# Seven of nine down products a slot, accumulated transposed from high and low parts

## What is computed

```
x = x + 0.5 * ffn_moe(layernorm(x))       # 16 experts of width 64, top 2, and a shared expert of width 128
x = x + linear_attention(layernorm(x))
x = x + 0.5 * ffn_moe(layernorm(x))       # the same weights again
x = x + 0.5 * ffn(layernorm(x))           # width 512, ReLU
```

```
g  = silu(einsum('th,ehi->eti', x, We_gate)); u = einsum('th,ehi->eti', x, We_up)
ye = einsum('eti,eih->eth', g * u, We_down)
y  = einsum('te,eth->th', comb, ye)
shared = silu(x @ Ws_gate) * (x @ Ws_up) @ Ws_down
```

## Time and profile before

| | |
|---|---|
| median of 3 runs | 1980.31 us (1979.03 to 1980.67) |
| the profiled execution, its own time | 1978.75 us |
| its span | 1976.9 us, granted TensorE clock 0.99 on the mean |
| the 32 slots with a side layer | from 70.62 to 1118.07 us of the span |
| the whole front | about the first 1146 us |

### The profile page before, as it was taken

One profiled execution on the slowest core, in us unless ns is written; L12 is line 12 of the kernel. 1 busy time (PEld: TensorE's weight loads), 2 busy tenths in 40 slices (PEclk: granted clock), 3 DMA queues, 4 the chain that ended last, 5 costly groups with the idle time before them and its releaser, 6 DMA issues. The chain is left out here.

```text
span 1976.9 us, 34600 instructions
## 1 busy us (share of the span) xinstructions
PE 1889.2 (96%) x12468; PEld 1308.3 (66%) x12468; DVE 1542.2 (78%) x3888; ACT 1179.2 (60%) x2210; POOL 670.7 (34%) x766
## 2 busy tenths in 40 slices
PE   2999999999999999999999979999999999999997
PEld 2888888888888888888888834444444444444443
DVE  5777776677767766776677679999999999999991
ACT  3344444444444444444444438888888888888884
POOL 2433433343234323432343223333333333333311
PEclk9999999999999999999999969999999999999998
DMA  3000000000000000000010032222222222223210
GB/s 132 7 11 1 12 11 12 1 12 12 12 1 11 12 12 1 12 12 11 1 38 7 6 102 87 87 87 89 91 91 89 90 88 87 87 88 90 87 40 11
DMA packets 49994, 85.83 MB, mean 43 GB/s; under 512 B 6753, under 2 KB 11105, under 8 KB 49761
## 3 DMA queue, kind: packets, MB, share of 16 engines
q1 hardware_dynamic: 47920, 81.85, 13.3%
q10 hardware_dynamic: 1904, 1.78, 0.3%
HBM read 49.26 MB, written 34.87 MB: 43 GB/s over the span
## 5 line engine op out<-in xcount | busy, mean ns | idle before, releaser
L1507 DVE TENSOR_REDUCE b_nm<-b_MX 128x1 f32<-128x512 f32 x1024 | 651.4, 682 | 45.1 <-PE b_MX L1615 27.1
L1400 ACT ACTIVATE b_pr<-b_ST 128x512 f32<-128x512 f32 x1024 | 552.3, 609 | 91.8 <-PE b_ST L1603 89.7
L517 ACT ACTIVATE s<-G 128x512 f32<-128x512 f32 x306 | 182.6, 597 | 293.7 <-PE G L836 289.5
L671 DVE TENSOR_TENSOR su<-U,s 128x512 f32<-128x512 f32 x272 | 187.0, 687 | 208.1 <-PE U L836 105.6
L841 PE MATMUL Y<-w_wd,h 128*128 128x128 f32 x2448 | 327.4, 277 | 4.3 <-DVE h L680 4.3
L841 PEld LDWEIGHTS Y<-w_wd,h 128*128 128x128 f32 x2448 | 308.1, 191 | 26.8 <-DVE h L680 14.7
L1615 PE MATMUL b_MX<-b_kt,b_qt 32*128 32x512 f32 x768 | 236.7, 504 | 2.4 <-DVE b_nm L1507 2.4
L1603 PE MATMUL b_ST<-b_qt,b_kt 32*128 32x512 f32 x768 | 214.7, 494 | 2.7 <-ACT b_pr L1400 1.5
L1603 PEld LDWEIGHTS b_ST<-b_qt,b_kt 32*128 32x128 f32 x768 | 83.1, 181 | 195.1 <-ACT b_pr L1400 140.3
L680 DVE TENSOR_TENSOR h<-C,su 128x512 f32<-128x512 f32 x272 | 188.0, 691 | 9.3
L834 PE MATMUL G<-xh,w_wgh 128*128 128x512 f32 x306 | 145.2, 475 | 0.0
(11 more groups left out here) (295 smaller groups left out, 3697.5 us busy)
## 6 DMA issues: line engine op xcount, KB each, us to landing
b_kt<-staging SPq DMA_DIRECT2D x48, 256.0 KB, 3.1
b_qt<-staging SPq DMA_DIRECT2D x48, 256.0 KB, 3.4
staging<-e_khi SPq DMA_DIRECT2D x32, 256.0 KB, 2.9
staging<-e_qhi SPq DMA_DIRECT2D x32, 256.0 KB, 2.9
xin<-in_x SPq DMA_DIRECT2D x17, 256.0 KB, 2.8
mid<-xo SPq DMA_DIRECT2D x16, 256.0 KB, 2.0
staging<-e_klo SPq DMA_DIRECT2D x16, 256.0 KB, 2.9
staging<-e_qlo SPq DMA_DIRECT2D x16, 256.0 KB, 2.9
```

What stands on the lines that cost most here:

```text
L517: nc.scalar.activation(sbuf_s[n % 2][:], G[n % 2][:], ACT.Silu).then_inc(act_done.sem, 1)
L671: nc.vector.tensor_tensor(out[:], U[:], sbuf_s[n % 2][:], ALU.mult).then_inc(up_used.sem, 1)
L1400: nc.scalar.activation(pr[k % 2][:, j], bank[:].rearrange("p a b -> p (a b)"), ACT.Exp, scale=SM_SCALE).then_inc(used["st"].sem, 1)
L1507: nc.vector.tensor_reduce(nm[g % 2][:, c:c + 1], bank[:].rearrange("p a b -> p (a b)"), AX.X, ALU.max).then_inc(used["mx"].sem, 1)
```

## The change

Tiles 0 to 6 (`NV` = 7) get another down product. ACT copies `h` into `hh` (float32r, the high part), POOL subtracts it, `hl = h - hh` (the low part), and PE adds three matmuls of 512 columns into a new PSUM bank `V`: `wdh` x `hh`, `wdl` x `hh`, `wdh` x `hl`. Here the weights are stationary, so `V` comes out transposed. After tile 6, ACT copies `V` to `vs`, and PE transposes that by four matmuls that accumulate onto `Y`, between the first and the second of the two down products (tiles 7 and 8) that stay as they were. `V` takes the bank of the second `G`, so that a gate product now waits for the `silu` of the tile just before it. Where the down products of tiles 0 and 1 stood in the loop's steps 1 and 2, there is none now; step 3 does tiles 0 and 1, step n from 4 to 7 does tile n - 2, and step 8 does tiles 6 and 7. DVE writes `h` for tile n once `hl` of tile n - 3 is done. The weights' parts `wdh` and `wdl` are made once, at the start.

```diff
+            def low(m, n, i):
+                pool.wait_ge(hh_ready.sem, hh_ready.at(i, NV * m + n + 1))
+                nc.gpsimd.tensor_tensor(hl[n % 3][:], h[n % 3][:], hh[n % 3][:],
+                                        ALU.subtract).then_inc(hl_ready.sem, 1)
...
                 for m in range(NM):
                     side_start(m, i, m)
-                    main_normalise(m + 1, i)
-                    if SIDE[m] == ATT:
+                    if SIDE[m] == MLP:
+                        lows(m, i, (0,))
+                        side_bias(m, i, m)
+                        lows(m, i, (1,))
+                        main_normalise(m + 1, i)
+                        lows(m, i, range(2, NV))
+                    else:
                         a = nth(m)
+                        lows(m, i, (0, 1))
+                        main_normalise(m + 1, i)
+                        lows(m, i, (2,))
+                        side_bias(m, i, m)
+                        lows(m, i, (3,))
...
+            lows(0, turns, range(4))
             pool.wait_ge(early.mv_ready.sem, 1)
...
+            def high(m, n, i):
+                if n == 0:
+                    act.wait_ge(up_used.sem, up_used.at(i, NT * m + 1))
+                else:
+                    act.wait_ge(h_ready.sem, h_ready.at(i, TE * m + n))
+                nc.scalar.activation(hh[n % 3][:], h[n % 3][:], ACT.Copy).then_inc(hh_ready.sem, 1)
...
+                    if 1 <= n <= NV:
+                        high(m, n - 1, i)
                     if n == 1 and side:
                         side_normalise(m, i, m)
...
                 if n >= 3:
-                    dve.wait_ge(down_done.sem, down_done.at(i, g0 + n - 2))
+                    dve.wait_ge(hl_ready.sem, hl_ready.at(i, NV * m + n - 2))
...
+                if n < NV:
+                    high, low = hh[n % 3], hl[n % 3]
+                    pe.wait_ge(hh_ready.sem, hh_ready.at(i, NV * m + n + 1))
+                    pe.matmul(flat(V), w["wdh"][:, n], flat(high), start=(n == 0), stop=False, skip_group_check=True)
+                    pe.wait_ge(hl_ready.sem, hl_ready.at(i, NV * m + n + 1))
+                    pe.matmul(flat(V), w["wdl"][:, n], flat(high), start=False, stop=False, skip_group_check=True)
+                    pe.matmul(flat(V), w["wdh"][:, n], flat(low), start=False, stop=True,
+                              skip_group_check=True).then_inc(down_done.sem, 1)
+                    return
...
-                    if n >= 1:
-                        moe_down(m, n - 1, i)
+                    if n == 3:
+                        moe_down(m, 0, i)
+                    if n >= 3:
+                        moe_down(m, n - 2, i)
+                    if n == NT - 1:
+                        moe_down(m, NT - 2, i)
...
                 if prepare:
                     gate(m + 1, 0, i)
+                down_transposes(m, i)
                 moe_down(m, NT - 1, i)
```

More of the change, by code:

```diff
@@ L34 @@
 NT = TE + 1
+NV = 7
 FT = 4
@@ L207, in build_front @@
         h = [sb(f"h{k}", [P, T, P]) for k in range(3)]
+        hh = [sb(f"hh{k}", [P, T, P], F32R) for k in range(3)]
+        hl = [sb(f"hl{k}", [P, T, P], F32R) for k in range(3)]
+        vs = sb("vs", [P, T, P])
         kvu = sb("kvu", [P, T, 3 * D])
@@ L225, in build_front @@
         hs = [sb(f"hs{k}", [P, T, P]) for k in range(2)]
-        G = [ps(f"G{k}", [P, T, P]) for k in range(2)]
+        G = ps("G", [P, T, P])
+        V = ps("V", [P, T, P])
         U = ps("U", [P, T, P])
@@ L399, in main_normalise, with lows, side_bias @@
                 nc.gpsimd.tensor_tensor(z[:], z[:], rstd[:].broadcast_to([P, T, D]), ALU.mult).then_inc(z_ready.sem, 1)
+            def low(m, n, i):
+                pool.wait_ge(hh_ready.sem, hh_ready.at(i, NV * m + n + 1))
+                nc.gpsimd.tensor_tensor(hl[n % 3][:], h[n % 3][:], hh[n % 3][:],
+                                        ALU.subtract).then_inc(hl_ready.sem, 1)
+            def lows(m, i, tiles):
+                for n in tiles:
+                    low(m, n, i)
             def side_start(m, i, k):
                 scale_offset(rstd_s, off_s, vpe_s, mv_s, smv_ready, smv_ready.at(i, k + 1), srstd_ready)
+            def side_bias(m, i, k):
                 pool.wait_ge(side_done.sem, side_done.at(i, k))
@@ L408, in _ @@
             main_normalise(-1, 0)
+            own.step(nc.gpsimd.tensor_tensor(w["wdl"][:], w["wd"][:, 0:NV], w["wdh"][:], ALU.subtract))
+            own.settle()
+            lows(-1, 0, (0, 1))
             main_normalise(0, 0)
+            lows(-1, 0, range(2, NV))
             own.step(nc.gpsimd.memset(early.va[:], 0.0))
@@ L454, in _ @@
             nc.gpsimd.tensor_tensor(early.xn[:], early.xn[:], w["lnsb"][:], ALU.add).then_inc(early.xn_ready.sem, 1)
+            lows(0, turns, range(4, NV))
         @block.scalar
@@ L516, in slot @@
                         act.wait_ge(up_used.sem, up_used.at(i, g0))
-                    nc.scalar.activation(sbuf_s[n % 2][:], G[n % 2][:], ACT.Silu).then_inc(act_done.sem, 1)
+                    nc.scalar.activation(sbuf_s[n % 2][:], G[:], ACT.Silu).then_inc(act_done.sem, 1)
                     if n == 0:
@@ L548, in slot @@
                         first_batch(n)
+                down_copy(m, i)
             main_high(-1, 0)
@@ L845, in moe_down, with down_transposes @@
             def moe_down(m, n, i):
-                if n == 0:
-                    pe.wait_ge(main_done.sem, main_done.at(i, m))
[L849 to L852, removed]
+                if n < NV:
[7 more added lines that the diff above has]
+                    return
+                if n == NV:
+                    pe.wait_ge(main_done.sem, main_done.at(i, m))
+                pe.wait_ge(h_ready.sem, h_ready.at(i, TE * m + n))
+                down(Y, h[n % 3], w["wd"][:, n], n == NV).then_inc(down_done.sem, 1)
+            def down_transposes(m, i):
+                pe.wait_ge(vs_ready.sem, vs_ready.at(i, m + 1))
+                for t in range(T):
+                    pe.matmul(Y[:, t], vs[:, t], w["ident"][:], start=False, stop=True, is_transpose=True,
+                              skip_group_check=True)
             def comb_transposes(m, i):
@@ L953, in gate @@
                 g0 = NT * m
-                if n >= 2:
-                    pe.wait_ge(act_done.sem, act_done.at(i, g0 + n - 1))
-                elif n == 0:
+                if n >= 1:
+                    pe.wait_ge(act_done.sem, act_done.at(i, g0 + n))
+                else:
                     pe.wait_ge(xl_ready.sem, xl_ready.at(i, m + 1))
@@ L1684, in build_weights @@
     sb("wd", [P, NT, D])
+    sb("wdh", [P, NV, D], F32R)
+    sb("wdl", [P, NV, D], F32R)
     for name in ("minus_half", "eps", "eps_two", "both"):
@@ L1819, in _ @@
                 nc.scalar.activation(high, whole, ACT.Copy).then_inc(high_ready, 1)
+            wait_loads(act, "down")
+            nc.scalar.activation(w["wdh"][:], w["wd"][:, 0:NV], ACT.Copy)
             for n, f in enumerate(angle):
```

11 lines of the change are left out of this document (10 added, 1 removed).

## The result

The changed kernel takes 2072.86 us (median of 4, 2069.65 to 2076.76), the kernel before on the same chip 1979.67 us (4, 1977.47 to 1980.67). The ratio is 1.047, with a 95% interval of 1.0453 to 1.0487: 4.7% slower. The profiled execution took 2073.94 us, with a span of 2072.1 us against 1976.9, so 95.2 us are to be found.

What follows compares the result with a forecast made beforehand. PE was taken to bound the kernel, busy 1032.77 of 1047.45 us in the 32 full slots. 16 x (3.0 + 0.6) + 16 x 0.8 + 9 = 79 us on 1978.75 gave 2058 us, range 2010 to 2100.

Steps and rivals of the forecast that it cites:

- PE saves 0.18 a product, 0.43 goes back: PE, every slot: seven cheaper down products save 1.27 us, four transposes onto `Y` cost 0.43; net 0.84 us.
- Nothing is saved up to step 3: ATT slot's start: PE reaches the transposes of `zs` sooner but must wait for the unchanged side-input chain; saving 0.
- `z` late by 2.34: ATT slot: `main_normalise` queues on POOL behind `hl` of tile 1, so PE waits for `z`; +2.34 us.
- The rest of the ATT slot: ATT slot, gate of tile 5 to next slot: +0.37 us of PE work, +0.6 (0 to 3.1) of DVE delays.
- MLP slot +0.8: MLP slot: tile 2's `V` product waits for `hl` behind `z`, more work follows; +0.8 us (0.4 to 1.3).
- Single `G` 0: Every step: the `silu` is over before the next gate product is due; cost 0, at worst 0.3.
- Last slot +8.9: Last slot: `e_xn`'s chain stands behind `hl` of tiles 0 to 3, +6.9 us, and slow clock afterwards, +2.
- Clock: ATT slots, a rival: the clock falls in every slot's pause, PE loses 2 us a slot; 2090 us, chance 0.06.
- Head and first slot at 0: Start: making `wdh`, `wdl` costs nothing; first slot loses about as much at `z` as PE saves; 0.
- Rival 1: All slots: PE's saving of 0.84 us a slot comes through, faster; about 1950 us, chance 0.04.
- Rival 2: `z` in time: POOL gets to `main_normalise` about when it did; ATT slot costs 0.7 us, total 2012, chance 0.14.
- the two SBUF terms: ATT slot: POOL's instructions hold up DVE's, the last `h` 0.5 us late and `en` ahead of `attend` 0.1.

Runs made afterwards that it cites:

- Experiment 8: Against the five-tile kernel of experiments 7: four tiles a slot through `V`, 2 to 5 in ATT slots, 3 to 6 elsewhere; 1960.19 us, 0.9899 of the kernel before.
- Experiment 2: Changed kernel with tile 0's three `V` matmuls moved from step 3 to step 2, ahead of the transposes of `zs`; 2059.43 us.
- Experiment 1: Changed kernel with POOL's low part of tile 1 moved behind `main_normalise` in ATT slots; 2028.19 us.
- Experiment 5: Changed kernel without POOL's subtractions in the slots, the third matmul of a product reading `hh` instead of `hl`; 1994.40 us.
- experiment 4: Kernel before with only one `G` bank, so a gate product waits for the `silu` of the tile just before it; 1979.38 us, ratio 0.9998.
- experiment 6: Changed kernel with POOL's chain of `e_xn` put ahead of all low parts in the last slot; 2070.29 us.
- Experiment 3: Changed kernel with six useless matmuls ahead of the transposes of `z` in ATT slots; 2059.55 us.
- experiments 7: Changed kernel with only tiles 2 to 6 through `V`, `z` made where it was before, `e_xn` ahead of the low parts; 1991.49 us, 1.0059 of the kernel before.
- experiment 9: Changed kernel, seven tiles, with the moves of Experiment 1, Experiment 2 and experiment 6 together; 2007.29 us, 1.0144 of the kernel before.

## Why the prediction was right, and where it was off

The forecast was 2058 us, slower, with 2010 to 2100; the measured 2072.86 lies inside, 15 us above the forecast.

- *PE saves 0.18 a product, 0.43 goes back.* The step of `V` is 0.235 us in the trace, as taken from the gate. Experiment 8, with PE waiting as before, gives 0.20 a product, with the 0.43 taken as given.
- *Nothing is saved up to step 3.* Right: the transposes of `zs` stand at tau 6.71. Experiment 2 shows the hole worth 0.70 us in an ATT slot and nothing in an MLP slot.
- *`z` late by 2.34.* `hl` of tile 1 starts at tau 7.64 (7.74 in the prediction) and `z` ends at 12.45 (12.6), and PE stands 2.04 us. Experiment 1 takes the wait away and 2.25 us a slot with it.
- *The rest of the ATT slot.* From the gate of tile 5 (tau 19.34) to the end are 16.61 us, 0.99 more than before; 0.37 + 0.6 = 0.97 was forecast. The wait for the last `h` is 0.41 us where 0.5 was taken. But both of DVE's instructions beside `hl` and `og` were caught, the case that the prediction priced at 1.8 us; that it cost no more than the case of one was luck. Experiment 5 shows POOL as their cause. Another 0.16 us stands in front of `S<-kvm,qc` (0.1 was forecast behind `en`); it is there without POOL's part too (experiments 5 and 8). The short ATT slot is 35.95 us, 36.0 by my sum.
- *MLP slot +0.8*: it is +0.70, with `z`'s transposes 0.24 us sooner and 0.34 us for tile 2's low part. *Single `G` 0*: experiment 4 shows it. *Last slot +8.9*: +9.2, and experiment 6 gets 6.5 of it back by order alone.
- *Clock: the term that was mis-sized.* I gave the fall of the clock as a rival, all or nothing, in every slot, at 2 us and a chance of 0.06, and put 0 into the sum. As a mechanism the rival was nearly right: the clock fell in 14 of 16 ATT slots. It cost only the 9 in which it fell behind `z`, 1.55 us each: 14 us. Experiment 3 fills the pause, with `z` as late as ever, and the cost is gone. My reason against it, that the pauses are short, rested on no row. The one longer pause in the front of before, 3.99 us in the first slot, could not have told: matmuls ran at 0.43 us a step ahead of it as well as behind it. A term between the two ends would have been due.
- *Head and first slot at 0* were mis-sized too, +3.6 us. The first slot (+1.1) now waits 0.71 us for `silu`, 0.34 us for a low part and 1.28 us for `z` (1.14 before), but in experiment 4, without any of the new work, it took 34.25 us too. The head is not settled: without the new parts of the weights it took 37.20 and 36.24 us (before, experiment 4), with them between 36.92 and 39.86 (nine kernels, mean 38.7), so the build looks like some 1.9 us, beside a spread of its own among kernels that start alike (37.13 to 39.74 in the change and experiments 1, 3 and 6). No run isolates either.

With the clock, and the head and first slot, 79 + 14 + 3.6 = 97 us, against 95.2.

Rival 1 (the saving comes through) broke on the `zs` chain: even without POOL's part the slots stay longer than before (experiment 5). Rival 2 (`z` in time) gave 2012; experiment 1 put `z` in time and got 2028. Rival 2 let the two SBUF terms go with the wait, and they stayed: ATT slots are 1.3 us over before, not 0.7 (10 us in all). The clock behind the stand at `zs` took another 5.6 (5 slots, 1.1 us each), and the rest is the head.

## What to carry to other kernels

On an engine that is 98% busy, mark the few places where it meets another engine's chain. Work that is made cheaper ahead of such a place saves nothing if the chain stands fixed; only what lies behind the last of them counts, and experiments 7 and 8 are the same idea on both sides of that line in MLP slots, where 21 of the 31 us between them lie (33.76 and 32.46 us). Of the ATT slots' 0.5 us, 0.41 is the wait for the last `h`, which went with tile 6, whose low part stood ahead of `og`. When a new instruction is put into an in-order queue, look at what is behind it, not at how busy the engine is: POOL was under 60% full and cost 78 us. And before a stall is priced by its own length, add the clock's fall behind it for some part of the cases, unless the next wait hides it.

## What the runs showed of the hardware

In the changed kernel's ATT slots PE stands twice, 1.34 us for `zs` (1.94 in the first) and then, about 4 us later, for `z`. In 5 of 16 slots the matmuls behind the first stand ran 0.43 us apart. In the other 11 the second stand was 2.03 to 2.05 us, and behind it they ran 0.43 us apart in 9, for up to 3.7 us, and 0.235 us apart in 2. In experiment 2, with no stand at `zs`, a pause of the same 2.04 us did it in 7 of 16. In experiments 1 and 5 the stand of 1.34 us alone did it, in 5 and in 4 of 16, and in experiment 9, with neither stand, none. What decides it from slot to slot these runs don't show. What a fall costs depends on what comes next: nothing where the next product has to wait for another engine anyway, 1.1 to 1.5 us where it has not. The Trainium skill's page TensorE: Matmul & The Clock Gate, section "Why this matters for your kernels", warns of idle gaps between bursts; the trace agrees that gaps do it, and shows it for gaps shorter than the one that the page names. Filling a pause with useless matmuls can therefore pay: 13.3 us here (experiment 3).
